# Stores of finished rows leave POOL's count of twelve transfers, and no pause stands directly ahead of one

## The chip, the cores and the metric

One core of one Trainium2 chip runs the program. The time is device microseconds of one execution; the kernel before took 1986.73 us, the median of three runs (1964.79, 1986.73 and 1987.19).

## The reference

The input is a matrix x of 8192 rows by 128 numbers and a 0/1 adjacency matrix adj of 8192 by 8192 (f32, 256 MB). One attention layer of four heads with 32 channels is computed over the edges, gated against a projection of the row itself, added to x and normalised:

```python
q, k, v = x @ Wq + bq, x @ Wk + bk, x @ Wv + bv        # 4 heads of 32
e = softmax over the keys m with adj[n, m] != 0 of (q[n] . k[m]) / sqrt(32)
out = sum over m of e * v[m]
x_r = x @ Ws + bs
beta = sigmoid(concat(out, x_r, out - x_r) @ Wb)
x = layernorm(x + beta * x_r + (1 - beta) * out)
```

The graph is sparse except for the first rows, and rows near the top have more neighbours than rows near the bottom.

## The kernel before

**Data.** The rows lie in 64 tiles of 128. Tile 0, which has many neighbours, is computed densely in small pieces beside the other work. Tiles 1 to 63 are computed sparsely: for every row a list of neighbours is made, and the keys and values of these neighbours are gathered from a table in HBM (`kv_rows`, 8193 rows of 1 KB, key and value side by side).

**Start.** Until about 66 us the kernel projects x to keys and values and stores the table, while POOL sets constants.

**Lists.** For every tile SyncE (SP) loads its 4 MB of adj in four parts of 1 MB (L603) into a ring of five. ScalarE (ACT) turns each part into a mask (L1023), TensorE (PE) packs the masks into words (L829), and VectorE (DVE) takes the largest words again and again (L1295) and decodes them to neighbour numbers (L1339). Tiles are handled in windows of eight; within one the rows are ranked by number of neighbours, and `scatter_records` (L766) writes each row's record (x, its list, its node number) to its place by rank with one indirect DMA for each tile. SP loads a tile's sorted record back (`load_record`, L610 to L616), four tiles ahead of its use; the record's slot is one of ten, and SP first waits until the finished rows of the tile ten before have been stored (`y_stored`).

**Units.** The loop of every engine runs over 76 units. A unit is a tile or a part of one, with up to 24 slots; slot s of a tile holds the s-th neighbour of each of its 128 rows. For each slot POOL issues one indirect DMA (L799), which gathers 128 rows of the table, 128 KB, into a slot of a ring of 60 (`s_kv`). DVE multiplies the keys by the query (L1246), reduces (L1248) and weighs the values (L1272) by ACT's exponentials; PE sums the weighted slots (L1001). Then DVE and ACT finish the rows of the tile, and ACT writes them to one of ten buffers (`y_out`, L1082, semaphore `y_ready`). POOL waits for a ring slot to be free through the semaphore `summed`.

**POOL's queue.** After the last gather of tile p, POOL issues the store of the finished rows of tile p - 6 (`store_rows`, L775), one indirect DMA that scatters 128 rows of 512 bytes to `out`. The last six stores follow the last gather. In all POOL issues 1148 indirect DMAs: 1023 gathers, 62 record scatters in eight groups, and 63 stores. Its program order is fixed.

**Pauses.** `pause_after(n)` counts the transfers begun since the last pause. Where n more would make over `RUN` = 12, POOL first waits until the gather that it issued last has landed, and the count begins anew. It is called with 1 ahead of each gather, with the number of tiles ahead of a group of record scatters, and with 1 ahead of each store.

**Fallback.** A loop for tiles whose lists would not hold runs once with these inputs: SP loads its data (L639 to L645) behind the record loads of unit 66, and PE, ACT and DVE take it at unit 65.

Of the kernel before, what the change touches and what calls it, by code (L numbers as in the profile page):

```python
# [268 lines left out]
def slots_landed(k):  # L269
    return 16 * sum(s for j, s in enumerate(HELD[:k + 1]) if j % FLIGHT == k % FLIGHT)  # L270
# [44 lines left out]
def sparse_tiles(nc, x, adj, Wq, bq, Wk, bk, Wv, bv, Ws, bs, Wb, kv_dram, x_cols, rec_dram, late_dram, ident, gate_w, eps_col, tile_list,  # L315
                 n_dense, n_late, w_all, b_row, bk_col, bq_col, ones, out):
    ctx = ExitStack()
    with ctx:
# [378 lines left out]
        def _(pool):  # L697
# [56 lines left out]
            def pause_after(n):  # L754
                if begun["since"] + n > RUN and begun["last"] is not None:
                    k, s = begun["last"]
                    pool.wait_ge(gathered[k % FLIGHT], slots_landed(k) - 16 * (HELD[k] - 1 - s))
                    begun["since"] = 0
                begun["since"] += n
# [10 lines left out]

            def store_rows(p):
                r = p % RECS
                pause_after(1)
                pool.wait_ge(y_ready, p)
                nc.gpsimd.indirect_dma_start(  # L775
                    out=out[:, :], out_offset=bass.IndirectOffsetOnAxis(ap=rec_in_u[:, r, NODE_AT:NODE_AT + 1], axis=0),
                    in_=y_out[:, r], in_offset=None,
                    bounds_check=last_node, oob_is_err=False).then_inc(y_stored[r], 16)
# [5 lines left out]
            for k, (p, c) in enumerate(UNITS):  # L784
                if k in SCATTER_AT:
                    scatter_records(SCATTER_AT[k])
                if c == 0 and p > 1:
                    pool.wait_ge(rec_loaded[p % RECS], rec_loads(p))
                for s in range(HELD[k]):
                    if s == 0 or FREE[k][s] > FREE[k][s - 1]:  # L790
                        need(pool, summed, FREE[k][s])
                    if p == 1 and (first_slot(1, c) + s) % 8 == 0:
                        pool.wait_ge(first_listed, (first_slot(1, c) + s) // 8 + 1)
                    col, n = LIST_AT + first_slot(p, c) + s, rows_with(p, first_slot(p, c) + s)
                    if s == plain(k):
                        col, n = FOLD_AT, P
                    pause_after(1)
                    begun["last"] = (k, s)
                    nc.gpsimd.indirect_dma_start(  # L799
                        out=kv[0:n, START[k] + s], out_offset=None, in_=kv_dram[:, :],  # L800
                        in_offset=bass.IndirectOffsetOnAxis(ap=rec_in_u[0:n, p % RECS, col:col + 1], axis=0),
                        bounds_check=last_row, oob_is_err=False).then_inc(gathered[k % FLIGHT], 16)
                if c == n_chunks(p) - 1 and p > BEHIND:
                    store_rows(p - BEHIND)
            for p in range(T - BEHIND, T):
                store_rows(p)
# [917 lines left out]
```

## Time and profile before

| | |
|---|---|
| median of three runs | 1986.73 us |
| the profiled execution's own time | 1964.78 us |
| its span in the trace | 1962.9 us |
| busy: PE, DVE, ACT, POOL | 1164.9, 1310.3, 839.9, 1174.4 us |
| granted TensorE clock, mean | 0.69 of full speed |
| DMA | 438.70 MB, mean 223 GB/s |

The profile is one execution. Busy time is that of instructions which compute or, on POOL, build an indirect DMA; an indirect DMA's landing is not part of it. "Idle before" is the time that an engine stood still ahead of an instruction, and its releaser is what ended this. "Issue" is time in which nothing that the profile shows was waited for. A pause of POOL appears in the trace as idle time released by the DMA into `s_kv`, in a few cases under "remote", "issue" or PE, whose semaphore came at about the same time. Of the three runs, the profiled one agrees with the lowest.

### The profile page before, as it was taken

The numbers are of one execution on the slowest core, as the hardware profiler recorded it, in microseconds if no ns is written. First come the engines' busy times: TensorE is split into PE (matmuls) and PEld (weight loads), VectorE is DVE, ScalarE is ACT, GpSimd is POOL, SyncE is SP. The second block draws the span as 40 slices with busy tenths as digits, with TensorE's granted clock in tenths as the row PEclk, the third lists the DMA queues.
The fourth block names the chain that finished last, engine by engine and source line by source line (L and its number), as shares of the span: only waits on it lengthen the run. The fifth ranks groups of instructions, "written<-read, shape, count | busy, mean of one in ns | idle before, by whom it ended". The sixth has DMA issues, their size and how long they took to land.

```text
span 1962.9 us, 20126 instructions
## 1 busy us (share of the span) xinstructions
PE 1164.9 (59%) x4696; PEld 680.4 (35%) x4696; DVE 1310.3 (67%) x3389; ACT 839.9 (43%) x1595; POOL 1174.4 (60%) x1711
## 2 busy tenths in 40 slices
PE   7322746657574756466655657756766668444553
PEld 5101433334342334233323334423423334233342
DVE  5876878666756776557656468757555677886564
ACT  2331443334643463344634348545635476431112
POOL 4454565566566656656566656565665665676664
PEclk9565677677776776667777578876667767666565
DMA  9947856666755776564866668776767778433331
GB/s 334 354 164 199 318 198 233 214 233 223 293 197 183 258 271 234 216 218 161 342 230 215 247 243 294 265 258 247 252 217 278 249 255 280 140 89 96 94 89 57
DMA packets 130037, 438.70 MB, mean 223 GB/s; under 512 B 26567, under 2 KB 61198, under 8 KB 97150
## 3 DMA queue, kind: packets, MB, share of 16 engines
q1 hardware_dynamic: 76510, 297.15, 41.1%
q0 software_dynamic: 52832, 136.07, 22.5%
q10 hardware_dynamic: 576, 4.19, 0.5%
q8 instruction: 38, 0.62, 0.1%
q14 instruction: 81, 0.66, 0.1%
HBM read 417.93 MB, written 19.44 MB: 223 GB/s over the span
## 4 chain that ended last, share of the span: by engine, by line
POOL 34%; issue 24%; DVE 13%; DMA 13%; PE 7%; DVEq 4%; another core or an unknown queue 3%; ACT 2%; SPq 1%; ACTq 0%; POOLq 0%
POOL s_kv L799 31%; DMA s_kv<-kv_rows,s_rec_in 11%; DVE s_raw L1248 2%; DVE s_kv L1246 2%; PE s_acc L1001 1%; DVEq L1296 1%; DVE s_wtop L1295 1%; POOL node_records L766 1%; POOL out_rows L775 1%; ACT s_mask L1023 1%; DVEq L1443 1%; DVE s_kv L1272 1%; DVE s_d_max L1454 1%; PE s_ps_key L889 1%
## 5 line engine op out<-in xcount | busy, mean ns | idle before, releaser
L799 POOL DMA_INDIRECT s_kv<-kv_rows,s_rec_in x1023 | 1024.3, 1001 | 700.6 <-DMA s_kv<-kv_rows,s_rec_in 340.6
L829 PE MATMUL s_ps_w<-s_mask,s_bit_w 128*128 128x512 bf16 x1008 | 374.6, 521 | 332.4 <-ACT s_mask L1023 233.8
L1023 ACT ACTIVATE s_mask<-s_adj_in 128x2048 bf16<-128x2048 f32 x252 | 478.2, 1900 | 114.5 <-DMA s_adj_in<-in_adj 66.7
L1001 PE MATMUL s_acc<-s_kv,ident 128*128 128x128 f32 x2032 | 321.3, 330 | 109.9 <-DVE s_kv L1272 62.8
L1001 PEld LDWEIGHTS s_acc<-s_kv,ident 128*128 128x128 f32 x2032 | 312.2, 244 | 137.4 <-DVE s_kv L1272 77.3
L829 PEld LDWEIGHTS s_ps_w<-s_mask,s_bit_w 128*128 128x128 bf16 x1008 | 111.3, 120 | 559.1 <-ACT s_mask L1023 294.9
L1246 DVE TENSOR_TENSOR s_kv<-s_kv,s_ps_q 128x1536 f32<-128x1536 f32 (+15 forms) x76 | 147.1, 1935 | 235.2 <-DMA s_kv<-kv_rows,s_rec_in 224.3
L1272 DVE TENSOR_TENSOR s_kv<-s_kv,s_ps_q 128x1536 f32<-128x1536 f32 (+15 forms) x76 | 146.7, 1931 | 17.9 <-ACT s_ps_q L1062 10.1
L1062 ACT ACTIVATE s_ps_q<-s_sc 128x56 f32<-128x56 f32 (+17 forms) x76 | 16.7, 220 | 318.4 <-DVE s_sc L1262 218.5
L1248 DVE TENSOR_REDUCE s_raw<-s_kv 128x48 f32<-128x1536 f32 (+15 forms) x76 | 147.1, 1935 | 5.6
L1050 ACT COPY s_xs<-s_ps_x 128x128 f32<-128x128 f32 x63 | 16.6, 264 | 288.7 <-remote 160.4
L889 PE MATMUL s_ps_key<-s_d_kT,s_d_qT 32*128 32x512 f32 x128 | 106.5, 924 | 51.5 <-DVE s_d_pen L1463 28.7
L1295 DVE MAX8 s_wtop<-s_words 128x8 f32<-128x512 f32 x171 | 118.8, 695 | 14.0 <-issue 0.4
L859 PE MATMUL s_ps_q<-b_row,ones 1*128 1x256 f32 x126 | 60.2, 568 | 94.2 <-ACT s_xs L1050 58.2
L775 POOL DMA_INDIRECT out_rows<-s_yout,s_rec_in x63 | 64.8, 1029 | 42.5 <-issue 18.5
L907 PE MATMUL s_ps_key<-s_d_v,s_d_wT 128*128 128x32 f32 x512 | 67.7, 277 | 25.8 <-issue 24.8
L766 POOL DMA_INDIRECT node_records<-s_rec,s_spot x62 | 61.8, 996 | 33.4 <-issue 17.6
L1339 DVE MAX8 s_top<-s_cand 128x8 f32<-128x72 f32 (+6 forms) x234 | 62.3, 266 | 29.1 <-issue 14.2
L1040 ACT ACTIVATE s_diag<-s_ps_key,s_neg_key 128x1024 bf16<-128x1024 f32 (+2 forms) x62 | 66.0, 1065 | 29.1 <-PE s_ps_key L844 24.9
L1454 DVE TENSOR_REDUCE s_d_max<-s_ps_key 128x1 f32<-128x1024 f32 x32 | 39.2, 1224 | 57.5 <-issue 20.6
L899 PE MATMUL s_ps_key<-ident,s_d_e 128*128 128x128 f32 x256 | 50.4, 362 | 45.6 <-ACT s_d_e L1093 36.7
L907 PEld LDWEIGHTS s_ps_key<-s_d_v,s_d_wT 128*128 128x128 f32 x512 | 66.2, 202 | 26.5 <-issue 25.3
(281 smaller groups left out, 1563.2 us busy)
## 6 DMA issues: line engine op xcount, KB each, us to landing
s_adj_in<-in_adj SPq DMA_DIRECT2D x248, 1024.0 KB
s_kv<-kv_rows,s_rec_in POOLq DMA_INDIRECT x1023
kv_rows<-s_kv SPq DMA_DIRECT2D x16, 512.0 KB, 7.6
s_rec_in<-node_records SPq DMA_DIRECT2D x55, 106.0 KB
s_kv<-in_x_cols SPq DMA_DIRECT2D x4, 1024.0 KB, 8.4
s_adj_in<-in_adj ACTq DMA_DIRECT2D x4, 1024.0 KB
s_d_in<-in_x_cols SPq DMA_DIRECT2D x8, 512.0 KB
s_d_v<-kv_rows SPq DMA_DIRECT2D x8, 512.0 KB
```

What stands on the lines that cost most here:

```text
L766: nc.gpsimd.indirect_dma_start(out=rec_dram[:, :], out_offset=bass.IndirectOffsetOnAxis(ap=spot[:, t:t + 1], axis=0), in_=rec[:, w % 2, j] ...
L775: nc.gpsimd.indirect_dma_start(out=out[:, :], out_offset=bass.IndirectOffsetOnAxis(ap=rec_in_u[:, r, NODE_AT:NODE_AT + 1], axis=0), in_=y_ ...
L799: nc.gpsimd.indirect_dma_start(out=kv[0:n, START[k] + s], out_offset=None, in_=kv_dram[:, :], in_offset=bass.IndirectOffsetOnAxis(ap=rec_i ...
L829: last = nc.tensor.matmul(w[:], bit_w[:, slab], mask[:, k % 2, s * WORD:(s + 1) * WORD], start=False, stop=(slab == SLABS - 1))
L889: nc.tensor.matmul(ps_key[:, b * 512:(b + 1) * 512], d_qT[h * C:(h + 1) * C, :], d_kT[h * C:(h + 1) * C, b * 512:(b + 1) * 512], start=Tru ...
L907: last = nc.tensor.matmul(ps_key[:, 0:C], d_wT[:, b * P:(b + 1) * P], d_v[:, b, h * C:(h + 1) * C], start=(b == 0), stop=(b == DKEYS // P ...
L1001: last = nc.tensor.matmul(acc[:, c * D:(c + 1) * D], ident[:], kv[:, START[k] + s, D:2 * D], start=(s == 0), stop=(s == plain(k) - 1))
L1023: nc.scalar.activation(mask[:, q % 2], adj_in[:, q % ADJ_RING], ACT.Sign, accum_out=edges[:, t, h:h + 1]).then_inc(masked, 1)
L1246: nc.vector.tensor_tensor(part, part, ps_q[r][:, 0:D].unsqueeze(1).to_broadcast([P, m, D]), ALU.mult)
L1248: nc.vector.tensor_reduce(raw[:, 0:m * H].rearrange("p (s h) -> p s h", h=H), part.rearrange("p s (h c) -> p s h c", h=H), AX, ALU.add)
L1272: last = nc.vector.tensor_tensor(v, v, e_sh.unsqueeze(3).to_broadcast([P, m, H, C]), ALU.mult)
L1295: nc.vector.max(got[:, 8 * k:8 * k + 8], words[:])
```

## The change

`store_rows` no longer calls `pause_after(1)`. A store is then neither counted, nor does POOL pause directly ahead of it; it still waits for `y_ready`. Gathers and record scatters are counted as before. Nothing else is altered, and each engine issues the same instructions in the same order, but for the waits.

```diff
--- before.py
+++ after.py
@@ -770,7 +770,6 @@
 
             def store_rows(p):
                 r = p % RECS
-                pause_after(1)
                 pool.wait_ge(y_ready, p)
                 nc.gpsimd.indirect_dma_start(
                     out=out[:, :], out_offset=bass.IndirectOffsetOnAxis(ap=rec_in_u[:, r, NODE_AT:NODE_AT + 1], axis=0),
```

## Rows read from the trace of the kernel before

**Rows 1.** The page's part 4: shares of the chain that ended last, by engine.
```profile
POOL 34%; issue 24%; DVE 13%; DMA 13%; PE 7%; DVEq 4%; another core or an unknown queue 3%; ACT 2%; SPq 1%; ACTq 0%; POOLq 0%
```

**Rows 2.** One line's instructions, L799 on POOL: durations in ns, minimum, median, maximum.
```profile
L799 POOL DMA_INDIRECT s_kv<-kv_rows,s_rec_in x1023: 892/998/1992, 66.5 to 1936.1; - x171
```

**Rows 3.** Waits of POOL, whole span: us in total, times, longest.
```profile
POOL s_kv L799 <- DMA s_kv<-kv_rows,s_rec_in: 340.6, 75, 18.0
...
POOL out_rows L775 <- DMA s_kv<-kv_rows,s_rec_in: 17.0, 5, 5.1
...
POOL node_records L766 <- DMA s_kv<-kv_rows,s_rec_in: 15.7, 5, 6.0
...
POOL out_rows L775 <- ACT s_yout L1082: 6.9, 2, 4.1
```

**Rows 4.** Timeline of POOL: start, us, instruction, idle before it and its releaser.
```profile
600.73 0.99 POOL L799 DMA_INDIRECT s_kv<-kv_rows,s_rec_in  x1 [6.20 <-DMA s_kv<-kv_rows,s_rec_in]
...
602.03 1.00 POOL L799 DMA_INDIRECT s_kv<-kv_rows,s_rec_in  x1 [0.30 <-issue]
...
618.10 1.00 POOL L799 DMA_INDIRECT s_kv<-kv_rows,s_rec_in  x1 [2.05 <-DMA s_kv<-kv_rows,s_rec_in]
...
1078.29 1.03 POOL L799 DMA_INDIRECT s_kv<-kv_rows,s_rec_in  x1 [1.09 <-issue]
```

**Rows 5.** Waits of POOL, 580.5 to 1043 us.
```profile
POOL s_kv L799 <- DMA s_kv<-kv_rows,s_rec_in: 92.8, 20, 6.4
...
POOL out_rows L775 <- DMA s_kv<-kv_rows,s_rec_in: 4.8, 2, 3.3
...
POOL s_kv L799 <- remote: 2.1, 1, 2.1
...
POOL node_records L766 <- DMA s_kv<-kv_rows,s_rec_in: 0.6, 1, 0.6
```

**Rows 6.** Waits of POOL, 1270.6 to 1352 us.
```profile
POOL s_kv L799 <- DMA s_kv<-kv_rows,s_rec_in: 18.3, 4, 6.2
```

**Rows 7.** Waits of POOL, 1672 to 1803 us.
```profile
POOL s_kv L799 <- DMA s_kv<-kv_rows,s_rec_in: 13.4, 6, 2.7
...
POOL s_kv L799 <- PE s_acc L1001: 2.1, 1, 2.1
...
POOL node_records L766 <- DMA s_kv<-kv_rows,s_rec_in: 1.1, 1, 1.1
```

**Rows 8.** Waits of POOL, 1889 to 1963 us.
```profile
POOL s_kv L799 <- DMA s_kv<-kv_rows,s_rec_in: 4.5, 2, 2.5
```

**Rows 9.** 2 us windows: busy us PE, PEld, DVE, ACT, POOL; clock, DMA share, GB/s.
```profile
594.53:596.53 2.00, 0.00 (x0) 0.00 (x0) 1.85 (x3) 0.00 (x0) 0.00 (x1) 0.50 1.01 406
...
1038.27:1040.27 2.00, 1.42 (x14) 1.25 (x12) 1.64 (x6) 1.72 (x2) 0.00 (x1) 1.00 0.67 178
...
601.72:603.72 2.00, 1.25 (x3) 0.15 (x1) 1.85 (x4) 1.93 (x7) 1.39 (x3) 0.64 0.99 391
...
1030.46:1032.46 2.00, 2.00 (x6) 0.76 (x5) 1.85 (x3) 0.51 (x3) 1.39 (x3) 0.50 1.00 393
```

**Rows 10.** Pieces of the chain that ended last: start, us, what.
```profile
1041.36 5.82 DMA s_kv<-kv_rows,s_rec_in
...
1270.46 1.00 POOL s_kv L799
...
1349.85 2.58 DMA s_kv<-kv_rows,s_rec_in
...
1805.58 0.50 SPq L571
...
1888.88 1.00 POOL s_kv L799
```

**Rows 11.** Waits of DVE, whole span.
```profile
DVE s_kv L1246 <- DMA s_kv<-kv_rows,s_rec_in: 224.3, 29, 19.5
...
DVE s_d_pen L1571 <- DMA s_d_v<-kv_rows: 9.1, 1, 9.1
```

## The prediction

> **What bounds the kernel now.** Read the chain of waits first: POOL and "issue" hold 58% of it, DVE 13%, DMA 13% [rows 1]. "Issue" here is mostly POOL too: between two transfers POOL stands still for 0.30 us, after 1.00 us of building [rows 2, 4]. So POOL goes at 1.30 us a transfer, 1148 x 1.30 = 1492 us, like a clock. What breaks the clock is the pauses: the waits of POOL for the landing of its own last gather add up to 340.6 + 17.0 + 15.7 = 373.3 us in 85 cases [rows 3]. Ring slots and finished rows hardly hold it: stores wait for ACT only in the tail, 6.9 us [rows 3].
>
> A pause has two prices. With no adj load in flight it is 2.05 us; under one it is 6.20 us, and when a store stands between the gather and the pause it is 1.09 us, since the store's 1.3 us cover a part of the landing [rows 4]. The DMA view shows what makes the dear ones: 406 GB/s at a share of 1.01 in the 2 us after a pause began [rows 9].
>
> POOL is not on the chain all the time. Followed from its start, the chain runs over POOL to 1041, over DVE, PE and ACT to 1270, over POOL to 1350, over ACT's masks, PE, DVE and adj loads to about 1672, over POOL to a store whose landing frees SP at 1805, over the fallback loop and DVE to 1889, and over POOL and DVE to the end [rows 10]. Pauses are worth their price only in the POOL stages.
>
> **The change part by part.** I stepped the counting rule through the 1148 transfers in order. Before, it pauses 97 times (85 ahead of a gather, 6 ahead of a store, 6 ahead of a group of scatters), and 91 of the 98 runs that they bound are of exactly 12 transfers. After, it pauses 91 times (86, 0 and 5), and of the 92 runs 42 are of 12, 41 of 13, 6 of 14 and 3 shorter. The first 25 pauses are the same, since no store has come by then. By stage:
>
> | stage, us | on the chain | pauses before | after |
> |---|---|---|---|
> | to 580 | POOL | 25 | 25 |
> | 580 to 1043 | POOL | 24 | 22 |
> | 1043 to 1270 | no | 12 | 12 |
> | 1270 to 1352 | POOL | 4 | 3 |
> | 1352 to 1672 | no | 16 | 15 |
> | 1672 to 1803 | POOL | 8 | 7 |
> | 1803 to 1889 | no | 5 | 4 |
> | 1889 to end | POOL | 3 | 3 |
>
> 580 to 1043: 24 pauses cost 92.8 + 4.8 + 2.1 + 0.6 = 100.3 us, 4.18 each [rows 5]. Two fewer at the mean are 8.4 us. But pauses also move, by one to eight transfers, and it matters whether they land in an adj load. Of the 24 old places, 12 have over 240 GB/s in the 2 us from the pause's start; of the 22 new ones, 8 (first and last of either list in [rows 9]). At 6.0 us for a busy place and 2.3 for a quiet one (what the 24 give when sorted so) the new ones would cost 8 x 6.0 + 14 x 2.3 = 80 us, 20 us less. The adj loads will not stay where they were, though, as ACT's masks follow the units, and in the old trace a gather at a new place often went into a queue that a pause had just emptied. I take 14, midway, and keep 8 and 20 as the ends.
>
> 1270 to 1352: 18.3 us for 4 pauses [rows 6], so one fewer is 4.6; between 2.05 and 6.2. 1672 to 1803: adj is loaded by then, and 13.4 + 2.1 + 1.1 = 16.6 us for 8 pauses are 2.08 each [rows 7]: 2.1. That gain comes through to the fallback, since DVE waits 9.1 us there for data that SP fetches only after POOL's store has landed [rows 10, 11]. 1889 to the end: as many pauses as before, but the last of the old ones stood ahead of a tail store long after its gather and cost nothing (two cost 4.5 us [rows 8]); the new three all stand ahead of gathers, one more at 2.05, a loss of 2.0.
>
> The stores that are no longer paused for still wait for `y_ready`. The cover of that wait is the six tiles between a store and its rows, and the two waits for ACT [rows 3] are both in the tail. If the cover goes, the gathers behind the store wait too. Earlier stores free SP's record loads earlier; that is a gain I price at nothing but for the 2.1 above. What is late next when POOL's stalls go is DVE's work. It waits for gathers 224.3 us in 29 cases over the span [rows 11], so it can follow a gain of this size where POOL is ahead of it on the chain, and nowhere else.
>
> The new thing is 53 transfers that are a run's 13th or 14th. The trace has no such place. Across places 2 to 12 a gather takes 1.00 us; the slowest one anywhere took 1.99 [rows 2]. I take 0 for the extra, nearest to the places that are there, and keep 0.99 as the upper bound. Below nothing it can't be.
>
> Sum: -14 - 4.6 - 2.1 + 2.0 = **-18.7 us**, from 1964.8 (the profiled execution's own time; its span is 1962.9, 1.9 us lie around it) to 1946.1. That execution agrees with the lowest of three runs; the other two took 22 us more, for reasons that one trace can't show. On the median of 1986.7 the same sum gives **1968 us**.
>
> One rule speaks against the gain. The 2 us window at 594.53 shows the DMA engines full under an adj load [rows 9], and the transfers that POOL would issue sooner go to those same engines. The Trainium skill, DMA: Bandwidth & Descriptors, "Issuing engines are not separate DMA queues", says that transfers from every issuer interleave on the same 16 engines, and that issuing more at once saves only the sequencer's time. By it the pauses in a load would give back nothing. Against that stands the span's mean of 223 GB/s beside the 406 of that window: the engines have room to catch up.
>
> **The rivals.**
>
> *A. The DMA engines set the pace, the pause only shows it.* If the queue's backlog under an adj load is served in its own time, a pause dropped there returns at the next one. Then each pause dropped pays its quiet price alone: 2 x 2.05 + 2.05 + 2.1 - 2.0, some 6 us, 1959, or 1980 on the median. For it: 6.20 against 2.05 [rows 4]. Against: loads come in bursts with gaps, and in a gap a backlog drains beside POOL's work.
>
> *B. Long runs are dear: slower than before.* Of the 53 transfers beyond the twelfth, 28 lie in POOL stages (12, 3, 8 and 5). If each costs 0.99 more (slower building, or a queue that must make room), that is 28 us: 1964.8 - 18.7 + 27.7 = 1974, or 1996 on the median. It decides from 18.7 / 28 = 0.67 us a transfer. Against it: twelve in a row show no growth at all. For it: nothing in the trace tells what a thirteenth would do.
>
> *C. The off-chain stage joins in.* 1352 to 1672 loses a pause and its places shift as well. If POOL's earlier stores there release SP's record and adj loads sooner, the pause comes through at 4.2 us, and with luck in the places three or four loads avoided at 6.0 - 2.3 = 3.7, some 13: -18.7 - 17 = -36, 1929, or 1951. Against: the chain there is ACT, PE and DVE.
>
> *D. The change does nothing that can be seen:* the moved pauses hit adj loads more often than the old ones, 4 more in the first stage at 3.7 us, 14.8, against 8.4 + 4.6 + 2.1 - 2.0 = 13.1 for the fewer pauses: 1966, or 1988. It is near A and shares its chance.
>
> **How the numbers follow.** Forecast 0.45; A with D 0.25; B 0.15; C 0.15. The median of a few runs may also fall on either side of a 22 us gap in the spread before, so the range runs from C's 1951 less some us to B's: 1943 to 1997; the likeliest case alone gives 1960 to 1976 (20 + 6.2 + 2.1 - 2.0 = 26, and 8.4 + 2.05 + 2.1 - 2.0 = 10.6). A measurement can tell about 2%, 40 us, from no change. Faster by over 2%, below 1947: part of C, and a low median of the forecast, 0.15. Slower by over 2%, above 2026: B at twice its bound, 0.04. Within: 0.81.
>
> **What would show it.** The waits of POOL for its gathers come in six cases less, and their sum over the span falls from 373.3 us by 25 to 45; transfers 13 and 14 of a run at 1.00 us with 0.30 between; 580 to 1043 shorter by 8 to 19 us; the last gather earlier by what the span loses. The forecast is wrong if the mean price of a pause rises so that the sum doesn't fall (A, D), if gathers beyond the twelfth take over 1.5 us (B), or if POOL's saving stands as a longer wait at 1270, 1672 or 1889 for `summed` or a record.

## The result: 1.1% slower where 0.95% faster was forecast

Over 20 runs of each, the changed kernel took 1983.05 us (median; 1954.39 to 2026.5) and the kernel before 1965.97 us (1929.25 to 1987.19). The ratio is **1.0114, with a 95% interval of 1.0072 to 1.0155**; the forecast was 1968/1986.7 = 0.9905. Here and below medians are of all runs of a kernel, while ratios and intervals leave out runs over 1.5% above the fastest of their kernel (slow runs), so that a ratio need not be the quotient of the medians, which here is 1.0087. The profiled execution after took 1970.68 us with a span of 1968.8, against 1964.78 and 1962.9. So the two traces lie 5.9 us apart and the two medians 17; the traces can explain the 5.9 at most.

**The chain.** The page after has this where [rows 1] stood:

```profile
POOL 26%; issue 23%; DVE 19%; DMA 10%; DVEq 6%; PE 6%; another core or an unknown queue 5%; ACT 4%; ACTq 0%; POOLq 0%
```

POOL's share fell from 34 to 26%, DVE's rose from 13 to 19%. "Another core or an unknown queue" rose from 3 to 5%. The program has one core, so this name means a release that no record accounts for. It is the name to follow below.

**POOL.** Next the line that answers to [rows 2]: durations of a gather in ns, minimum, median, maximum.

```profile
L798 POOL DMA_INDIRECT s_kv<-kv_rows,s_rec_in x1023: 897/1002/1952, 67.3 to 1929.1; - x171
```

The last gather was issued at 1929.1 instead of 1936.1: POOL is 7 us earlier, and the span ends 6 us later. These waits of POOL over the span (us, times, longest) answer to [rows 3]:

```profile
POOL s_kv L798 <- DMA s_kv<-kv_rows,s_rec_in: 345.8, 78, 16.1
...
POOL node_records L766 <- DMA s_kv<-kv_rows,s_rec_in: 22.6, 5, 5.5
POOL out_rows L774 <- ACT s_yout L1081: 22.3, 5, 6.2
```

The waits for a gather add up to 345.8 + 22.6 = 368.4 us, 4.9 less than the 373.3 of before, where the prediction asked for 25 to 45 less. The wait for finished rows grew from 6.9 to 22.3 us. The stage with the largest term, 580.5 to 1031 us, answers to [rows 5]:

```profile
POOL s_kv L798 <- DMA s_kv<-kv_rows,s_rec_in: 77.5, 20, 7.0
...
POOL node_records L766 <- DMA s_kv<-kv_rows,s_rec_in: 4.3, 1, 4.3
...
POOL s_kv L798 <- PE s_acc L1000: 2.5, 1, 2.5
POOL s_kv L798 <- remote: 2.2, 1, 2.2
```

That is 86.5 us where there were 100.3. The tail after the last gather looks like this in POOL's timeline (start, us, [idle before]):

```profile
1929.07 1.00 POOL L798 DMA_INDIRECT s_kv<-kv_rows,s_rec_in  x1 [0.30 <-issue]
...
1936.02 0.98 POOL L774 DMA_INDIRECT out_rows<-s_yout,s_rec_in  x1 [3.30 <-ACT s_yout L1081]
1943.25 0.98 POOL L774 DMA_INDIRECT out_rows<-s_yout,s_rec_in  x1 [6.25 <-ACT s_yout L1081]
1950.05 0.98 POOL L774 DMA_INDIRECT out_rows<-s_yout,s_rec_in  x1 [5.82 <-ACT s_yout L1081]
...
1958.93 0.98 POOL L774 DMA_INDIRECT out_rows<-s_yout,s_rec_in  x1 [4.14 <-ACT s_yout L1081]
```

From the last gather to the end are 40 us, before 27. POOL had run ahead, and the rows of the tiles behind it were not finished.

**Who was late.** For some units, the end of the unit's last gather on POOL and the start of DVE's multiplication (L1245, before L1246), from the two timelines:

| unit | before: gather, DVE | after: gather, DVE |
|---|---|---|
| 31 | 1018, 1020 | 1006, 1008 |
| 59 | 1662, 1710 | 1664, 1699 |
| 63 | 1752, 1766 | 1741, 1776 |
| 67 | 1812, 1852 | 1807, 1860 |
| 71 | 1894, 1896 | 1887, 1910 |
| 75 | 1937, 1940 | 1930, 1946 |

At unit 31 DVE follows POOL within 2 us and the change has gained 12 us. From unit 59 on DVE is tens of us behind its data in both kernels. Before, it had caught up by unit 71; after, it never did. (The lag at unit 67 is mostly the fallback loop's, which stands before it: it is 36 us in the trace of an unchanged copy, below, that has no late releases.) A part of what held DVE shows in PE's and ACT's timelines of the kernel after. In each pair PE transposes a record into `s_ps_x`, and ACT copies it out:

```profile
1708.35 0.42 PE L850 MATMUL s_ps_x<-ident,s_rec_in 128*128 128x128 f32 x1
...
1895.76 0.27 PE L850 MATMUL s_ps_x<-ident,s_rec_in 128*128 128x128 f32 x1
```

```profile
1724.45 0.27 ACT L1049 COPY s_xs<-s_ps_x 128x128 f32<-128x128 f32 x1 [9.70 <-remote]
...
1905.21 0.27 ACT L1049 COPY s_xs<-s_ps_x 128x128 f32<-128x128 f32 x1 [15.11 <-remote]
```

The copies began 15.68 and 9.18 us after the transposes' recorded end (1708.77 and 1896.03), with ACT idle for the last 9.70 us of the first and throughout the second. ACT's waits and work before that explain neither: what it waited for had been recorded as done. I call such a handoff **held** where ACT had stood idle for over 0.3 us and the copy began more than 1.5 us after the end of its transpose. The trace after has 20 of them, 140 us in all, the longest 16. The trace before has 20 as well, 143 us, the longest 18. So they aren't new; the prediction had passed them over. In the last 69 us of the trace after, 17.7% of the chain is "another core or an unknown queue", and no gather of POOL's has a part in it; in the last 69 us of the trace before, gathers and their landings have 17.2%.

### The profile page after: what moved, and what is told of

Its sections match the earlier page's. It is cut to its first block, busy times and chain, and to the rows that moved or that the text cites. A ratio compares the mean times of both kernels' runs of the same rounds, so it can differ in the third digit from the quotient of the medians.

```text
span 1968.8 us, 20057 instructions
## 1 busy us (share of the span) xinstructions
PE 1132.9 (58%) x4636; PEld 663.8 (34%) x4696; DVE 1311.0 (67%) x3389; ACT 839.0 (43%) x1595; POOL 1177.3 (60%) x1711
## 4 chain that ended last, share of the span: by engine, by line
POOL 26%; issue 23%; DVE 19%; DMA 10%; DVEq 6%; PE 6%; another core or an unknown queue 5%; ACT 4%; ACTq 0%; POOLq 0%
POOL s_kv L798 24%; DMA s_kv<-kv_rows,s_rec_in 9%; DVE s_raw L1247 3%; DVE s_kv L1245 2%; DVEq L1295 2%; DVE s_wtop L1294 2%; POOL node_records L766 1%; ACT s_mask L1022 1%; PE s_acc L1000 1%; DVEq L1442 1%; DVE s_d_max L1453 1%; DVE s_top L1338 1%; DVE s_kv L1271 1%; PE s_ps_w L828 1%
## 5 line engine op out<-in xcount | busy, mean ns | idle before, releaser
L798 POOL DMA_INDIRECT s_kv<-kv_rows,s_rec_in x1023 | 1027.4, 1004 | 697.9 <-DMA s_kv<-kv_rows,s_rec_in 345.8
L1000 PE MATMUL s_acc<-s_kv,ident 128*128 128x128 f32 x2032 | 307.7, 320 | 88.0 <-issue 47.9
L1000 PEld LDWEIGHTS s_acc<-s_kv,ident 128*128 128x128 f32 x2032 | 298.0, 234 | 113.3 <-issue 59.4
L1245 DVE TENSOR_TENSOR s_kv<-s_kv,s_ps_q 128x1536 f32<-128x1536 f32 (+15 forms) x76 | 147.2, 1936 | 221.5 <-DMA s_kv<-kv_rows,s_rec_in 203.3
L1049 ACT COPY s_xs<-s_ps_x 128x128 f32<-128x128 f32 x63 | 16.6, 263 | 279.8 <-remote 158.2
L888 PE MATMUL s_ps_key<-s_d_kT,s_d_qT 32*128 32x512 f32 x128 | 100.3, 873 | 56.8 <-DVE s_d_pen L1462 34.8
L906 PE MATMUL s_ps_key<-s_d_v,s_d_wT 128*128 128x32 f32 x512 | 73.3, 282 | 51.3 <-issue 46.4
L906 PEld LDWEIGHTS s_ps_key<-s_d_v,s_d_wT 128*128 128x128 f32 x512 | 71.7, 211 | 51.6 <-issue 44.7
L774 POOL DMA_INDIRECT out_rows<-s_yout,s_rec_in x63 | 64.5, 1024 | 40.0 <-ACT s_yout L1081 22.3
L766 POOL DMA_INDIRECT node_records<-s_rec,s_spot x62 | 61.9, 999 | 41.9 <-DMA s_kv<-kv_rows,s_rec_in 22.6
L1290 DVE MATCH_REPLACE8 s_words<-s_wtop,s_words 128x512 f32<-128x512 f32 x108 | 73.0, 676 | 0.0
L858 PEld LDWEIGHTS s_ps_q<-b_row,ones 1*128 1x128 f32 x126 | 24.1, 237 | 136.7 <-ACT s_xs L1049 98.9
```

Of the source, the lines that this page charges most:

```text
L798: nc.gpsimd.indirect_dma_start(out=kv[0:n, START[k] + s], out_offset=None, in_=kv_dram[:, :], in_offset=bass.IndirectOffsetOnAxis(ap=rec_i ...
L858: nc.tensor.matmul(ps_q[p % 2][:, 0:2 * D], ones[:], b_row[0:1, 2 * D:4 * D], start=True, stop=False)
L888: nc.tensor.matmul(ps_key[:, b * 512:(b + 1) * 512], d_qT[h * C:(h + 1) * C, :], d_kT[h * C:(h + 1) * C, b * 512:(b + 1) * 512], start=Tru ...
L906: last = nc.tensor.matmul(ps_key[:, 0:C], d_wT[:, b * P:(b + 1) * P], d_v[:, b, h * C:(h + 1) * C], start=(b == 0), stop=(b == DKEYS // P ...
L1000: last = nc.tensor.matmul(acc[:, c * D:(c + 1) * D], ident[:], kv[:, START[k] + s, D:2 * D], start=(s == 0), stop=(s == plain(k) - 1))
L1245: nc.vector.tensor_tensor(part, part, ps_q[r][:, 0:D].unsqueeze(1).to_broadcast([P, m, D]), ALU.mult)
```

## The experiments

Kernels of one sitting ran on one chip beside the kernel before. The result above is the first sitting; the trace that the prediction was made from is older, and its three runs are among the 20 of the kernel before. A sitting is called prompt where none of its traces has a held handoff.

**Second sitting: the change again, its halves, and runs of 14**

The change alone, once more:

> The changed kernel once more, for a second trace of it. In the first one POOL did issue its last gather 7 us earlier than before (1929.1 against 1936.1 us), no transfer beyond the twelfth was dear (1.015 us each), and yet the span was 6 us longer: from the last gather to the end it took 40 us in place of 27. Theory L (long runs): 13 or 14 transfers in a row cost something that shows later; this kernel is 1% slower again and the dear place can be found. Theory P (places): the time depends on where the pauses fall against the units and the adj loads, not on their number; again 1% slower, as the places are the same. Theory C (other chain): POOL no longer sets the end; VectorE again lags some 15 us behind the last gathers, where before it lagged 2.

Measured: 1949.17 against 1975.17 us, **0.9866 [0.9833, 0.99]**. The sign is the other one, and the two intervals are far apart. Its chain, by engine, and POOL's waits:

```profile
POOL 50%; issue 23%; DMA 16%; PE 4%; DVE 4%; DVEq 1%; ACT 1%; SPq 0%; POOLq 0%; ACTq 0%
```

```profile
POOL s_kv L798 <- DMA s_kv<-kv_rows,s_rec_in: 360.6, 85, 15.6
...
POOL node_records L766 <- DMA s_kv<-kv_rows,s_rec_in: 19.2, 5, 5.4
```

POOL holds 50% of the chain and no unknown queue is on it; the waits for a gather are 379.8 us.

One half: a store is not counted, but still paused for where a pause is due.

```diff
                 pause_after(1)
+                begun["since"] -= 1
```

> Only the first half of the change: a store is not counted, but POOL still pauses ahead of it where twelve transfers have gone. The same 91 pauses and the same lengths of runs as in the changed kernel; eight pauses stand ahead of a store in place of directly behind it, and cost up to 1.3 us more each. Theory L: as slow as the change, 1.01 of the time before, since the runs are as long. Theory P: anything between 0.99 and 1.02. If the second half of the change did the harm, 0.99, which was my forecast for the whole.

Measured: 1955.05 us, 0.9885 [0.9847, 0.9922], with 91 pauses, as many as the whole change has.

The other half: a store is counted, but no pause stands ahead of it.

```diff
-                pause_after(1)
+                begun["since"] += 1
```

> Only the second half of the change: a store is counted, but POOL takes no pause directly ahead of it. 96 pauses in place of 97, 83 runs of 12, seven of 13 and one of 17. Theory L: no change beyond 0.3%, since hardly a run is longer. Theory P: most pauses stay where they are, so 0.995 to 1.005. If the second half did the harm, 1.01.

Measured: 1967.4 us, 0.9959 [0.9932, 0.9986], with 96 pauses; 7 runs have 13 transfers and one has 17. Both halves gain, and the first is most of it. Moved places and longer runs are in both and cost nothing that can be seen in this sitting; whether they do where releases are held, this sitting can't tell.

Longer runs everywhere, the stores counted and paused for as before:

```diff
-RUN = 12
+RUN = 14
```

> The kernel before with runs of 14 in place of 12, stores counted and paused for: 83 pauses in place of 97, so 14 fewer, more than twice what the change takes away, and 80 runs of 14. Theory L: slower than the change, 1.02 or more. By my forecast's arithmetic (3 to 4 us a pause, two thirds of them on the chain) 0.98. Theory C: the same as before within 0.5%, since POOL's time no longer counts.

Measured: 1909.38 us, **0.9662 [0.9629, 0.9695]**, with 83 pauses, 80 of its runs being 14 long. 65.8 us for 14 pauses fewer are 4.7 each. Runs of 14 are not dear by themselves.

**Third sitting: is it the sitting, and how far does it go?**

> The changed kernel a third time, in another session. First result: ratio 1.011 over 20 runs of each, second 0.987 over 6 against 17. Theory V (the variation lies between sessions, not in the change): a third ratio between 0.98 and 1.015, that may fall on either side, with a narrow spread inside the session. Theory F (my forecast holds and the first session was the exception): 0.985 to 0.992 again. Theory L (long runs dear) is already against the second session and would need 1.01.

Measured: 1947.49 against 1972.65 us, 0.9892 [0.9857, 0.9927].

The kernel before, unchanged, as a kernel of its own:

> The kernel before, unchanged, timed as if it were a new one against itself, for a second trace of it and for what a fresh load of the same program does to the time. If a load fixes the time within a session (addresses, say), its ratio differs from 1 by up to 1% though nothing is changed; if not, it is within 0.3% of 1.

Measured: 1973.79 us, 1.0012 [0.9991, 1.0032]; the comparison has no bias. Its trace is the most useful of all, since it is the same program as the trace that the prediction was made from. ACT's waits for `s_xs` and their largest releasers, first in the trace of the prediction, then in this copy:

```profile
ACT s_xs L1050 <- remote: 160.4, 19, 20.2
ACT s_xs L1050 <- PE s_ps_x L851: 104.4, 24, 27.2
```

```profile
ACT s_xs L1050 <- PE s_ps_x L851: 155.8, 34, 27.2
```

The copy has no held handoff at all (the 27.2 us are a wait of ACT for a transpose that came late itself). One and the same transpose of the program shows it, in the timelines of PE and of ACT, first in the trace of the prediction:

```profile
1298.76 0.31 PE L851 MATMUL s_ps_x<-ident,s_rec_in 128*128 128x128 f32 x1
```

```profile
1309.17 0.27 ACT L1050 COPY s_xs<-s_ps_x 128x128 f32<-128x128 f32 x1 [9.57 <-remote]
```

and in that of the copy:

```profile
1300.06 0.31 PE L851 MATMUL s_ps_x<-ident,s_rec_in 128*128 128x128 f32 x1
```

```profile
1300.40 0.27 ACT L1050 COPY s_xs<-s_ps_x 128x128 f32<-128x128 f32 x1 [0.67 <-PE s_ps_x L851]
```

10.10 us against 0.03. POOL's timeline is alike in both around it: transfers of 1.00 us with 0.30 between, then a wait for a landing, which began 1.76 us before the held copy did.

The traces also keep the times of the semaphores' updates. In the 20 held handoffs of the trace before and the 20 of the trace after, the update is recorded 0.02 us before the copy began, and not at the end of the transpose; without a hold it stands 0.01 us behind that end. So by the records ACT answered at once, and PE's update came late.

And PE's own work stands still as well. After one held transpose of the trace of the prediction PE's eight matmuls that pack words were spread over 10.5 us:

```profile
1446.30 0.37 PE L851 MATMUL s_ps_x<-ident,s_rec_in 128*128 128x128 f32 x1 [1.23 <-issue]
...
1447.73 1.01 PE L829 MATMUL s_ps_w<-s_mask,s_bit_w 128*128 128x512 bf16 x2 [0.63 <-issue]
...
1457.66 0.59 PE L829 MATMUL s_ps_w<-s_mask,s_bit_w 128*128 128x512 bf16 x1 [1.52 <-issue]
```

The same eight in the copy:

```profile
1467.93 1.89 PE L829 MATMUL s_ps_w<-s_mask,s_bit_w 128*128 128x512 bf16 x8
```

The granted clock was 0.50 in the first stretch and 1.00 in the second (1.2 and 2.4 GHz), but a lower clock is the smaller part: eight such matmuls at a mean of 0.53 took 3.64 us in a trace without holds. Over the span PE stands idle under "issue" or "remote" for 279.5 us in the trace of the prediction and for 44.4 in the copy. In all traces of this case it is 257 to 579 us where copies are held and 44 to 46 where none is.

No pauses at all:

```diff
-RUN = 12
+RUN = 10000
```

> The kernel before with no pause at all: POOL waits only for ring slots, records and finished rows. Runs of 14 in place of 12 gave 0.966, so fewer pauses paid more than my price for them (14 pauses, 66 us). Theory F: POOL saves up to 400 us of pauses, but VectorE, with 1310 us busy, and ACT and PE behind it bound the kernel long before; 0.88 to 0.94. Theory L: somewhere beyond 14 the queue clogs and a transfer takes longer than 1.3 us; then no better than 0.97, or slower than before.

Measured: 1658.88 us, **0.8411 [0.8385, 0.8437]**. The 97 pauses had cost 313.8 us, 3.2 each; DMA moved 265 GB/s on the mean instead of 223.

> The kernel before with runs of 24: 48 pauses in place of 97. Theory F: 0.90 to 0.94. Theory L: the transfers 15 to 24 of a run take over 1.3 us each, and the time is above that with runs of 14, 0.966.

(`RUN = 24`.) Measured: 1784.6 us, 0.9048 [0.9021, 0.9075], with 48 pauses: 3.8 us for each of the 49 dropped.

**Fourth sitting: the places of the pauses, and no pauses once more**

> The changed kernel in a fourth session. Two later sessions gave 0.987 and 0.989, the first 1.011. In the first session's two traces ACT waits some 400 us under 'issue' and 'remote', that is for releases which no record explains; in the six traces since it is 3 us. Theory S (the first session was in a state of its own, with late releases between PE, ACT and VectorE, in which VectorE's chain and not POOL's sets the end): where a trace shows the late releases the ratio is 1.00 to 1.015, where it does not it is 0.985 to 0.992. Theory V (sessions scatter by themselves): the ratio is not tied to these waits.

Measured: 1979.47 against 1966.46 us, **1.0081 [1.0038, 1.0124]**. The slower sign is back, and with it the held handoffs: 23, 201 us, the longest 28. "Another core or an unknown queue" has 7% of the chain, and the tail stores wait 35.2 us for ACT.

The kernel before with every pause moved: its count begins at 4, then at 8.

```diff
-            begun = {"since": 0, "last": None}
+            begun = {"since": 4, "last": None}
```

> The kernel before with its count begun at 4 in place of 0: 97 pauses as before, but most of them four transfers earlier in the program. Places, not number. My forecast took 6 to 12 us for places leaving adj loads. If places matter that much, 0.99 to 1.01 with an interval clear of 1; if a pause has one mean price wherever it stands, within 0.3% of 1.

> The same with the count begun at 8: 98 pauses, eight transfers earlier. One more pause at its mean price of 4 us is 1.002; places can move it to either side by up to 1%.

Measured: 1970.89 us, 1.0012 [0.9975, 1.0049], and 1964.81 us, 1.0034 [0.9991, 1.0077], with 97 and 98 pauses. By either interval a mere move of the pauses costs less than 0.8%; 32 and 28 copies of `s_xs` are held.

> The kernel without pauses in another session: 0.84 again if it was no matter of the session. In a session with late releases it should be worse, since VectorE's chain would set the end: 0.86 to 0.90.

The kernel that took 1658.88 us took 2158.68: **1.0966 [1.0903, 1.1028]** where it had been 0.8411. First the chain and one handoff (PE's transpose, ACT's copy) of its run in the third sitting:

```profile
DVE 33%; POOL 22%; issue 13%; DVEq 11%; PE 8%; DMA 8%; ACT 4%; SPq 1%; ACTq 0%; POOLq 0%
```

```profile
875.26 0.27 PE L851 MATMUL s_ps_x<-ident,s_rec_in 128*128 128x128 f32 x1
```

```profile
875.57 0.27 ACT L1050 COPY s_xs<-s_ps_x 128x128 f32<-128x128 f32 x1 [0.97 <-PE s_ps_x L851]
```

Then the same of this run, the same transpose of the program:

```profile
DVE 29%; issue 21%; PE 15%; another core or an unknown queue 14%; DVEq 11%; ACT 7%; DMA 1%; ACTq 1%; POOL 0%; POOLq 0%; SPq 0%
```

```profile
1088.23 0.27 PE L851 MATMUL s_ps_x<-ident,s_rec_in 128*128 128x128 f32 x1 [2.57 <-issue]
```

```profile
1115.21 0.27 ACT L1050 COPY s_xs<-s_ps_x 128x128 f32<-128x128 f32 x1 [30.74 <-remote]
```

0.04 us against 26.71. POOL has 0% of the chain here, and the holds stand among DVE's waits as well:

```profile
DVE s_divisor L1425 <- remote: 150.6, 13, 22.5
DVE s_d_max L1454 <- remote: 75.4, 8, 19.9
DVE s_d_max L1454 <- PE s_ps_key L891: 62.9, 9, 35.5
```

The handoff from DVE to ACT (`s_d_e`) is late in no trace of either kind, 0 of 30 to 32 in each. From ACT to PE (the weight load behind ACT's copy of the turned exponentials) PE was idle for it only 64 times in the nine traces with holds, and in 4 of these it began 2.5 to 8.9 us late, under "issue". So it is mostly what PE releases that comes late, and PE itself that stands still.

**Fifth sitting: is it POOL's break, or its wait for a landing?**

The pause replaced by eight small chained memsets, about 1.5 us of work on POOL without an issue, at the same 97 places:

```diff
-                    k, s = begun["last"]
-                    pool.wait_ge(gathered[k % FLIGHT], slots_landed(k) - 16 * (HELD[k] - 1 - s))
+                    for _ in range(8):
+                        nc.gpsimd.memset(idle[:], 0.0).then_inc(idled, 1)
+                        begun["idled"] += 1
+                        pool.wait_ge(idled, begun["idled"])
```

> The kernel before, but each of its 97 pauses waits for no landing: POOL does eight tiny memsets, each waiting for the one before, about 1 to 1.5 us, and goes on. In sessions of the first kind (no late releases) a pause then costs 1 to 1.5 us in place of 4.1, so some 270 us less, and as POOL runs ahead the other engines take a part back: 0.86 to 0.90. In sessions of the second kind (TensorE's releases come late while POOL issues, and arrive some 2 us after POOL stops) it tells what sets them free. Theory R (any break in POOL's issuing does): they arrive soon after each memset break, the holds are as long as before and the time falls to 0.90 to 0.97. Theory W (it is the wait, or the landing, that frees them): as without pauses, 1.05 to 1.10.

Measured: 2066.64 against 1963.18 us, 1.0542 [1.0489, 1.0595]. The chain has "another core or an unknown queue 16%", and ACT's copy waits as long as without any pause (228.9 here, 245.0 there):

```profile
ACT s_xs L1054 <- remote: 228.9, 15, 36.4
```

So breaks of this length do not bring the releases as the waits for a landing do. Counted over the three kinds of handoff from PE (`s_xs`, `s_d_wT`, `s_d_max`): of the 30 held ones of the trace after, 21 ended 1.6 to 2.6 us after POOL had begun to stand still, in the fourth sitting's run of it 24 of 37, in the trace of before 10 of 24, with the shifted counts 18 of 40 and 18 of 36, and in the two runs below 3 of 16 (runs of 8) and 19 of 41 (runs of 14): 113 of 224 together. With memsets it is 7 of 40, with no pauses 6 of 39. Only 5 to 7% of the span lies in such a stretch of the traces with waits, so that half of the releases fall there is no accident. But it is only half, and 22 of the 224 holds lasted through a whole wait of POOL.

The question put is not answered by this, though. The 97 memset breaks lasted 1.52 us at the median, the waits for a landing 4.0 (the trace after), and a release came 1.6 to 2.6 us after POOL had stopped: most memset breaks were over by then. A longer break without a wait was not tried, so that it is the landing, and not the length of the break, is not shown.

> The kernel before with runs of 8: 147 pauses in place of 97. In a session of the first kind, 50 more at 3.2 to 4.7 us are 160 to 235 us: 1.08 to 1.12. In one of the second kind the holds are shorter, 8 x 1.3 = 10 us at most, and give a part of that back: 1.04 to 1.09.

(`RUN = 8`.) Measured: 2071.99 us, 1.0585 [1.0518, 1.0651], with 147 pauses. Holds are fewest here, 13 and 104 us for `s_xs`, but 50 more pauses cost more than they give. The longest, 22.2 us, is longer than a run of eight transfers: POOL waited for a landing in the middle of it.

> Runs of 14, stores counted, 83 pauses. In a session of the first kind 0.966 again. In one of the second kind, theory R: the 14 pauses saved give 60 us on POOL, but TensorE's releases are held up to 18 us in place of 16, and the changed kernel with runs of 12 to 14 is already 1% slower: 0.99 to 1.02.

Measured: 1948.16 us, **0.9849 [0.9768, 0.993]**, where the second sitting gave 0.9662. This ratio rests on two of four runs, which lie between 1922.84 and 1965.32 us; the medians of all runs give 0.9923. So a gain is likely and not shown, and a loss was not seen. Its trace (of an execution of 1960.68 us) has 19 held copies, 177 us, and 11% of its chain under "another core or an unknown queue".

**Sixth sitting: the halves beside the whole**

> The change as it is, a fifth time, beside its two halves on one chip. On the chips where TensorE's releases reach ScalarE and VectorE in 0.04 us: 0.987 to 0.989 as twice before. On those where they come up to 28 us late: 1.008 to 1.011 as twice before. Anything between, with late releases in the trace, says that the two kinds are not two.

> Half of the change: a store is not counted but still has a pause directly ahead of it where one is due; the program pauses as often as the whole change does. On a chip without late releases: 0.9885 as before. On one with them: Theory N (the number of POOL's waits sets how long releases are held) says as the whole change, 1.005 to 1.012, since both have 91. Theory S (what hurts is that stores go out without a pause ahead) says 0.99 to 1.00 here and leaves the loss to the other half.

> The other half: stores are counted, but no pause is taken directly ahead of one, 96 pauses against 97. On a chip without late releases: 0.996 as before. On one with them: Theory N says 1.00 within 0.004, since the number is almost the same; Theory S says 1.005 to 1.012, the whole loss.

Measured, against 1976.29 us: 1947.23, 0.9857 [0.9828, 0.9885]; 1952.24, 0.9881 [0.9858, 0.9905]; 1962.36, 0.9932 [0.9909, 0.9955]. No trace of the three has a held handoff. So the halves stand confirmed for sittings in which releases are prompt, and the question put to this one, which half costs where releases are held, has no answer. Nor is it a matter of the chip's number: the fourth and the sixth sitting list the same one and are of different kinds.

**The sittings side by side**, ratios to the kernel before:

| | prompt (2nd, 3rd, 6th) | with held releases (1st, 4th, 5th) |
|---|---|---|
| the change | 0.9866, 0.9892, 0.9857 | 1.0114, 1.0081 |
| runs of 14 | 0.9662 | 0.9849 (medians 0.9923) |
| no pauses | 0.8411 | 1.0966 |
| held copies of `s_xs` | 0 in all 11 traces | 13 to 32 in 9 traces |

The kernel before itself takes about the same in both, 1973 to 1976 and 1963 to 1966 us. That is why its median did not give the kind away. Its spread did: from lowest to highest 13 to 21 us in the prompt sittings, 31 to 58 in the others.

PE's idle time and the held copies split the 20 traces in the same way. So does a third thing, the records themselves: of the updates of the semaphores that DVE and ACT raise, 1370 to 1372 are on record in each of the 11 prompt traces and 910 to 1068 in the 9 others, and 8 of the 9 have 4636 matmuls of PE where all the rest have 4696, though the program issues as many. That leaves a rival which no run here tests: that taking the records is part of what holds PE in these sittings.

## Why the prediction was wrong

**What held.** POOL's stalls (gaps over 0.5 us between two transfers) by the stages of the prediction, cut at the same transfers; the right column is the copy of before and the fifth run of the change, both from prompt sittings:

| stage, us | forecast | before, after | prompt: before, after |
|---|---|---|---|
| to 580 | 0 | 134.4, 132.3 | 126.0, 122.5 |
| 580 to 1043 | -14 | 100.3, 86.4 | 98.9, 89.4 |
| 1043 to 1270 | 0 | 48.8, 56.8 | 56.6, 56.2 |
| 1270 to 1352 | -4.6 | 18.4, 14.5 | 18.1, 17.8 |
| 1352 to 1672 | 0 | 73.4, 74.0 | 79.2, 75.0 |
| 1672 to 1803 | -2.1 | 16.6, 17.7 | 15.9, 13.9 |
| 1803 to 1889 | 0 | 12.4, 8.5 | 12.2, 8.7 |
| 1889 to end | +2.0 | 13.2, 29.0 | 14.6, 15.2 |
| sum | -18.7 | +1.7 | -22.8 |

The spans moved by +5.9 and by -23.9 us. (The second and third run of the change, prompt as well, have 390.6 and 396.7 us of stalls, 31 and 25 less than the copy's 421.6.) In the prompt pair the sum comes out with the right sign and about the right size, but in part by luck: the four stages that had a price gave -9.5 - 0.3 - 2.0 + 0.6 = -11.2 us where -18.7 was said, and the four that were priced at nothing gave -11.6. Of those, -3.5 before 580 is scatter, since the first 25 pauses are the same. The -4.2 of 1352 to 1672 and the -3.5 of 1803 to 1889 are a pause each, in stages off the chain in the trace that was read; between 1352 and 1672 the copy's chain is POOL and its landings throughout. That is rival C's first half, at its price of 4.2; its 13 us from places did not come.

**The transfers beyond the twelfth** were priced at 0, and cost 0. The 47 thirteenth and 6 fourteenth ones of the kernel after took 1.015 and 1.010 us, and the gaps ahead of them 0.31. Rival B, slower by dear long runs, has the sign that was measured, but not by its mechanism, and runs of 14 and 24 refute it again. For pauses in prompt sittings rival A is refuted as well: six pauses fewer gave 25 to 29 us in three sittings, where it said some 6.

The prediction weighed a rule of the Trainium skill, DMA: Bandwidth & Descriptors, "Issuing engines are not separate DMA queues". The section says that DMAs of every issuer run on the same 16 engines, and that starting them from several engines at once saves only the sequencer's time. That a transfer issued sooner by the same engine would give back nothing was the prediction's own step from there, and the runs are against it: without pauses the engines moved 265 GB/s on the mean over a span of 1657.0 us, instead of 223.

**The step that failed** is this one: "What is late next when POOL's stalls go is DVE's work. It waits for gathers 224.3 us in 29 cases over the span, so it can follow a gain of this size where POOL is ahead of it on the chain". It took DVE's slack at the mean over the span. In the trace that it was read from, DVE ran behind its data at units 59, 63 and 67, by 48, 15 and 40 us. In the copy, without held releases, it is 12, 2 and 36 us, so most of the lag at unit 67 is there anyhow, and most of that at 59 and 63 comes with the held releases; DVE waits 342.8 us in 45 cases there for the same data. After the change, POOL arrived 7 us earlier and DVE 14 us later at unit 71 (1887 for 1894, 1910 for 1896), and the tail's +2.0 became +15.8. The wait that took the place of the saving is that for `y_ready` in the tail, 22.3 us for 6.9. The prediction had named this cover, and priced its loss at nothing; of the three places where it said that a saving could come back as a wait, 1889 was the right one, for another semaphore.

The other part of the failure lies within POOL's own ledger, the term for the fewer pauses: the 97 pauses of the trace before take 400.5 us and the 91 of the trace after 392.1, so six fewer brought only 8.4 us, 1.4 each. The stage from 1043 to 1270 lost 8.0 us with the same 12 pauses, 4.7 each for 4.1. This looks like what rival D says, but it is not shown: of the change and the kernels with the same 12 pauses or nearly the same there, ten other traces have 52.5 to 61.5 us in this stage, so the 48.8 of the trace before is what stands apart, and two prompt traces have 56.6 before and 56.2 after.

**What was there to see.** [Rows 1] has "another core or an unknown queue 3%" in a program of one core, and the profile of before had 160.4 us of ACT's `s_xs` under "remote". The prediction took no notice of either. A look at how long after its transpose the copy began would have shown 20 handoffs of up to 18 us, and with them that another chain stood close behind POOL's.

**Shown and not shown.** Shown: the change gains in the three prompt sittings that had it and loses in the two with held releases, and in these POOL's last stores wait 22.3 and 35.2 us for finished rows, and 8.6 to 8.7 in the prompt ones. Shown too: dropping every landing wait gives 16% or costs 10%, by the kind of sitting alone. Only argued: that the loss of 0.8 to 1.1% comes from POOL waiting six times less. Against it stands `RUN = 14`, which waits 14 times less and shows no loss there, and the shifted counts, with 32 and 28 held copies to the change's 20 and 23 and no loss that can be told from none (nor, with 1.0034 [0.9991, 1.0077], quite from the change's). Held time summed over a trace does not order the kernels; so it presumably matters where a hold falls, in the last 200 us above all, where nothing is left to catch up; this is argued from the tail and not tested. Open: what makes a sitting one kind or the other; why PE stands still and its releases are held while POOL issues indirect DMAs, and why half of them come about 2 us after POOL starts to wait for a landing; which half of the change does the harm. Whether releases are held in an execution of which no records are taken is shown by nothing here, and the missing records make it a rival to be taken seriously.

The Trainium skill, Perfetto Trace Analysis, "Tensor Engine Instruction (MATMUL, LD_WEIGHTS)", says that the end shown for a matmul is computed, and that its semaphore update is pushed and becomes visible after it. The prompt traces agree, with 0.03 to 0.04 us for both together. Against that stand the held ones with up to 26.71 us in the pair shown. As the update is recorded just before the copy, what was late lies between the computed end and the recorded update; whether the matmul itself ended late or only its update, no record tells.

## What to carry to other kernels

Before an engine's stalls are priced, subtract the end of a producer from the start of its idle consumer, handoff by handoff: a release that is late by more than a fraction of a us marks a second chain that the busy shares don't show. So does idle time of PE under "issue", 44 us in one kind of sitting and over 257 in the other. A throttle that looks like pure cost (3 to 5 us a pause) may be what keeps another engine going, so judge its removal in more than one sitting. Of the kernels tried in both kinds, runs of 14 gain in one and were not seen to lose in the other; no pauses is best in one and worst in the other.

## What the runs showed of the hardware

- In nine traces a release by PE reached an idle ACT (the copies into `s_xs`) up to 31 us after the transpose's recorded end, while POOL issued indirect DMAs, in some cases through a wait of POOL as well. In eleven other traces, of the same programs for a part, it took 0.1 us at most. DVE's release to an idle ACT (for `s_d_e`) took 0.04 us at most in all 20.
- In the same nine traces PE stood idle for 257 to 579 us with nothing on record that it waited for, in the eleven for 44 to 46.
- POOL went at the same 1.00 + 0.30 us a transfer in both kinds, with pauses after 12, 14 or 24 transfers and with none.
- The mean granted clock was 0.74 of full speed in the fastest run and 0.675 in the slowest, both without pauses, and PE was busy 1075.8 and 1163.8 us in them.
